# Wide attention of a four-layer block: the order of the front, of the first eight units and of GpSimd's loads rearranged

## The reference

```python
q = rms_norm((x @ wq).reshape(B, L, 16, 128), q_norm_w)
k = rms_norm((x @ wk).reshape(B, L, 4, 128), k_norm_w)
v = (x @ wv).reshape(B, L, 4, 128)
k_ctx = rms_norm((h_ctx_kv @ wk_ctx).reshape(B, T, 4, 128), k_norm_w)
v_ctx = (h_ctx_kv @ wv_ctx).reshape(B, T, 4, 128)
...
```

## Time and profile before

| | |
|---|---|
| median of 3 runs | 1155.62 us (1152.46 to 1157.61) |
| the profiled execution | 1157.82 us, its span 1155.9 us |
| PE busy | 1049.1 us (91%) |
| PE weight loads busy | 847.5 us (73%) |
| DVE busy | 700.8 us (61%) |
| ACT busy | 503.6 us (44%) |
| POOL busy | 232.1 us (20%) |
| mean granted clock of TensorE | 0.972 |

### The profile page before, as it was taken

One profiled execution on the slowest core, in us unless ns is written; L12 is line 12 of the kernel. 1 busy time (PEld: TensorE's weight loads), 2 busy tenths in 40 slices (PEclk: granted clock), 3 DMA queues, 4 the chain that ended last, 5 costly groups with the idle time before them and its releaser, 6 DMA issues.

```text
span 1155.9 us, 23193 instructions
## 1 busy us (share of the span) xinstructions
PE 1049.1 (91%) x9488; PEld 847.5 (73%) x9488; DVE 700.8 (61%) x1337; ACT 503.6 (44%) x867; POOL 232.1 (20%) x356
## 2 busy tenths in 40 slices
PE   6899999989999879999987889989999999999885
PEld 3655678865666645677765668889999999999763
DVE  3646242347777358888643766765665566667466
ACT  3042221125666338888754523333233232232374
POOL 4501038402132000000010411210100133332030
PEclk9998999997999979999999989999999999999898
DMA  9711246554663517000141200131111112100000
GB/s 381 292 72 62 87 153 230 182 140 115 181 180 100 170 39 249 3 2 2 38 147 37 92 25 31 37 110 41 53 37 38 55 58 79 57 19 10 1 2 10
DMA packets 39188, 104.57 MB, mean 90 GB/s; under 512 B 4144, under 2 KB 12720, under 8 KB 37424
## 3 DMA queue, kind: packets, MB, share of 16 engines
q1 hardware_dynamic: 35184, 91.55, 24.2%
q0 software_dynamic: 2752, 9.44, 2.4%
q10 hardware_dynamic: 1152, 2.16, 0.5%
HBM read 87.93 MB, written 15.20 MB: 89 GB/s over the span
## 4 chain that ended last, share of the span: by engine, by line
PE 72%; DVE 13%; ACT 4%; issue 4%; POOL 4%; DMA 2%; DVEq 0%; SPq 0%; POOLq 0%; ACTq 0%
PE ps L2225 9%; PE ps L433 7%; PE ps L2180 7%; PE ps L1413 5%; PE ps L1764 5%; PE ps L426 4%; PE ps L2070 4%; PE ps L488 3%; PE ps L1755 3%; PE ps L1561 3%; PE ps L2084 2%; PE ps L1091 2%; PE ps L1099 2%; PE ps L1572 2%; DVE st L1690 2%
## 5 line engine op out<-in xcount | busy, mean ns | idle before, releaser
L2225 PE MATMUL ps<-vv,prob 128*128 128x129 f32 x1024 | 128.7, 274 | 0.0
L2225 PEld LDWEIGHTS ps<-vv,prob 128*128 128x128 f32 x1024 | 122.5, 192 | 0.0
L1690 DVE TENSOR_REDUCE st<-ps 128x1 f32<-128x512 f32 x128 | 83.5, 687 | 27.3 <-PE ps L1561 21.1
L2348 DVE TENSOR_REDUCE probT<-ps 128x128 f32<-128x1024 f32 x64 | 82.6, 1290 | 28.4 <-PE ps L2180 20.4
L2115 ACT ACTIVATE kt<-ps,w 128x512 f32<-128x512 f32 x32 | 22.1, 689 | 141.8 <-PE ps L2092 141.8
L433 PE MATMUL ps<-xT,big 128*128 128x256 f32 x352 | 79.8, 381 | 1.4 <-ACT xT L715 0.7
L2360 DVE TENSOR_TENSOR prob<-ps,probT 128x1024 f32<-128x1024 f32 x64 | 79.6, 1286 | 1.1
L2321 ACT ACTIVATE prob<-prob 128x1024 f32<-128x1024 f32 x64 | 70.8, 1107 | 19.6 <-DVE prob L2360 19.5
L1637 ACT ACTIVATE prob<-ps 128x1024 f32<-128x1024 f32 x64 | 65.8, 1030 | 28.7 <-PE ps L1572 27.0
L152 POOL TENSOR_SCALAR small<-small 128x4 f32<-128x4 f32 (+1 forms) x44 | 12.0, 273 | 325.7 <-DVE small L2122 175.3
L433 PEld LDWEIGHTS ps<-xT,big 128*128 128x128 f32 x352 | 66.4, 190 | 11.8 <-DVE prob L504 1.9
(11 more groups left out here) (456 smaller groups left out, 2216.1 us busy)
## 6 DMA issues: line engine op xcount, KB each, us to landing
big<-ctxT_in SPq DMA_DIRECT2D x36, 512.0 KB, 4.1
big<-blocks_in SPq DMA_DIRECT2D x22, 768.0 KB, 4.4
key_parts<-w POOLq DMA_DIRECT2D x16, 384.0 KB, 5.0
kt<-key_parts SPq DMA_DIRECT2D x32, 192.0 KB, 3.3
vv<-ctx_in SPq DMA_DIRECT2D x2, 2176.0 KB, 27.3
vv<-early_values SPq DMA_DIRECT2D x4, 1088.0 KB, 12.1
kt<-ctxT_in SPq DMA_DIRECT2D x2, 2048.0 KB, 13.2
kt<-key_parts SPq DMA_DIRECT2D x32, 128.0 KB, 3.2
```

Of the source, the lines that this page charges most:

```text
L1690: dve.tensor_reduce(self.mx[:, u % 2, n:n + 1], k.ps[:, n % 2, :], AX.X, ALU.max).then_inc(s("reduced"), 1)
L2225: last = pe.matmul(k.ps[:, 7, 0:DH + 1], self.prob(u)[:, ch * P:ch * P + P], v, start=(ch == 0), stop=(ch == MC))
L2348: dve.tensor_reduce(self.largest[:, h * P:(h + 1) * P], bank.rearrange("p (c t) -> p t c", t=P), AX.X, ALU.max).then_inc(s("c3_max"), 1)
```

## The change

It touches only the class `Wide` and two functions of `Eight`.

- In the front, key product 4 goes to bank 3 and ahead of the turned keys 0, which move to bank 6; turned heads 4 go ahead of turned keys 2. ScalarE scales heads 1 before the squares 0 and 1; VectorE rotates pieces 3 and 4 earlier and normalizes keys 4 in the front and not in unit 0; GpSimd's order follows.
- In unit 0 turned keys 4 and the projection go ahead of the turning and spreading of the largest scores, the key product behind them; the scores' last four blocks wait for the normalized keys 4 (bank 3).
- In `between_tensor` the values go behind the wait for `w_kt`, and behind the projection where there is one. In units 1 and 4 half of them stay ahead; in TURN_AT's units the turned heads go ahead of the wait; in units 6 and 7 the key product goes ahead of the values.
- ScalarE's order in units 0 to 7 follows (scaling at the unit's start, copy of turned heads behind the key copy, value copy behind the second exp).
- GpSimd's load of the rounded weights' next piece goes behind the root.

```diff
@@ front_tensor
-        self.turn_keys(pe, 0, 3)
-        self.key(pe, 4, 6)
+        self.key(pe, 4, 3)
+        self.turn_keys(pe, 0, 6)
         self.turn_keys(pe, 1, 7)
         pe.wait_ge(s("w_q"), 1)
         self.turn_heads(pe, 0, 3, 0)
-        self.turn_keys(pe, 2, 4)
         pe.wait_ge(s("w_q"), 2)
         self.turn_heads(pe, 0, 4, 1)
+        self.turn_keys(pe, 2, 4)
         self.turn_keys(pe, 3, 5)
@@ scores
+            if u == 0 and ch == 12:
+                pe.wait_ge(s("w_kn"), self.FRONT)
@@ turn_last_output
-        elif u - 1 in self.TURN_AT:
-            pe.wait_ge(s("w_q"), 5 + self.TURN_AT[u - 1] + 1)
@@ between_tensor
-        if g not in self.FIRST_VALUES:
-            self.value(pe, g, 5)
+        if u in self.TURN_AT:
+            self.turn_heads(pe, 1, self.TURN_AT[u], 5)
+        elif u in (1, 4):
+            self.value(pe, g, 5, range(0, 2))
         pe.wait_ge(s("w_kt"), g)
         if u < 6:
             self.project(pe, 1, u, 6)
+        if u == 0:
+            self.turn_largest(pe, u)
+            self.spread_largest(pe, u)
+        if u in (6, 7):
+            self.key(pe, g, 6)
         if u in self.TURN_AT:
-            pe.wait_ge(s("w_v_sb"), g + 1)
-            self.turn_heads(pe, 1, self.TURN_AT[u], 5)
+            pe.wait_ge(s("w_q"), 5 + self.TURN_AT[u] + 1)
+        if u >= 1:
+            self.value(pe, g, 5, range(2, 4) if u in (1, 4) else range(4))
         if u < 6:
             pe.wait_ge(s("w_heads"), 6 + u + 1)
-        self.key(pe, g, 6)
+        if u not in (6, 7):
+            self.key(pe, g, 6)
@@ scalar, the front
+        self.scale_heads(act, 0, 1)
         self.square(act, 0, 6)
         self.square(act, 1, 7)
         self.copy_turned(act, 0, 0, 0)
-        self.scale_heads(act, 0, 1)
-        self.square(act, 2, 4)
         self.copy_turned(act, 0, 1, 1)
         self.scale_heads(act, 0, 2)
+        self.square(act, 2, 4)
         self.square(act, 3, 5)
         self.copy_turned(act, 0, 2, 2)
-        self.copy_keys(act, 0, 3)
         self.scale_heads(act, 0, 3)
-        self.square(act, 4, 6)
+        self.square(act, 4, 3)
+        self.copy_keys(act, 0, 6)
         self.copy_keys(act, 1, 7)
         self.copy_turned(act, 0, 3, 0)
         self.scale_heads(act, 0, 4)
+        self.copy_turned(act, 0, 4, 1)
         self.copy_keys(act, 2, 4)
-        self.copy_turned(act, 0, 4, 1)
         self.copy_keys(act, 3, 5)
@@ scalar, the units
+            if self.TURN_AT.get(u, 0):
+                self.scale_heads(act, 1, self.TURN_AT[u])
             if u >= 2:
                 self.copy_output(act, u - 2, P)
             if g - 1 < self.GROUPS:
                 self.copy_keys(act, g - 1, 6)
-            if self.TURN_AT.get(u, 0):
-                self.scale_heads(act, 1, self.TURN_AT[u])
+            if u in self.TURN_AT:
+                self.copy_turned(act, 1, self.TURN_AT[u], 5)
+            if u == 0:
+                self.copy_heads(act, 1, u, 6)
             if u < self.UNITS:
                 exp(u, 0)
-            if g < self.GROUPS and g not in self.FIRST_VALUES:
+            if u in (6, 7):
+                self.square(act, g, 6)
+            if 1 <= u < 6:
+                self.copy_heads(act, 1, u, 6)
+            if u >= 8 and g < self.GROUPS:
                 self.copy_value(act, g, 5)
             if u < self.UNITS:
                 exp(u, 1)
-            if g < self.GROUPS:
-                if u < 6:
-                    self.copy_heads(act, 1, u, 6)
-                if u in self.TURN_AT:
-                    self.copy_turned(act, 1, self.TURN_AT[u], 5)
+            if 1 <= u < 8:
+                self.copy_value(act, g, 5)
+            if g < self.GROUPS and u not in (6, 7):
                 self.square(act, g, 6)
@@ vector, the front
-        for n in range(3):
+        for n in range(4):
             self.rope(dve, o, 0, n)
         self.sum_squares(dve, 0)
         self.sum_squares(dve, 1)
-        self.rope(dve, o, 0, 3)
+        self.rope(dve, o, 0, 4)
         for g in range(2):
             self.normalize(dve, g, self.key_bank(g))
         self.sum_squares(dve, 2)
         self.sum_squares(dve, 3)
-        self.rope(dve, o, 0, 4)
         for g in range(2, 4):
             self.normalize(dve, g, self.key_bank(g))
         self.sum_squares(dve, 4)
+        self.normalize(dve, 4, self.key_bank(4))
@@ gpsimd
             self.scales(pool, o, g)
+            if u >= self.EIGHT_AT:
+                eight.weights_load(pool, dram, u - self.EIGHT_AT + 2)
```

More of the change, by code:

```diff
@@ L1904 @@
     FIRST_VALUES = (0, 4, 1, 5, 2, 3)
-    KEY_BANKS = (6, 7, 4, 5, 6)
+    KEY_BANKS = (6, 7, 4, 5, 3)
     def __init__(self, k):
@@ L2072, in key, with value @@
         last.then_inc(k.s("w_k"), 1)
-    def value(self, pe, g, bank):
+    def value(self, pe, g, bank, tiles=range(4)):
         k, (b, h, i) = self.k, self.place(g)
@@ L2081, in value @@
         pe.wait_ge(k.s(f"w_stage{slot}"), 16 * loads)
-        for t in range(4):
+        for t in tiles:
             for c in range(DC):
@@ L2085, in value @@
                                  self.ctx("wv_ctx", DC)[:, c, h * DH:(h + 1) * DH], start=(c == 0), stop=(c == 1))
-        last.then_inc(k.s("w_v"), 1)
+        if t == 3:
+            last.then_inc(k.s("w_v"), 1)
     def turn_keys(self, pe, g, bank):
@@ L2275, in tensor @@
                 self.product(pe, u - 1, range(0, 9))
-            if u < self.UNITS:
+            if 1 <= u < self.UNITS:
                 self.turn_largest(pe, u)
@@ L2380, in vector @@
                 self.largest_of(dve, u, 0)
-            if u + F - 1 < self.GROUPS:
+            if F <= u + F - 1 < self.GROUPS:
                 self.normalize(dve, u + F - 1, self.key_bank(u + F - 1))
@@ L2413, in gpsimd @@
         self.ones(pool, o)
-        for n in (1, 2):
+        for n in (1, 2, 3):
             self.query_scales(pool, o, 0, n)
@@ L2417, in gpsimd @@
             self.scales(pool, o, g)
-            if g % 2:
-                self.query_scales(pool, o, 0, 3 + g // 2)
+            if g == 1:
+                self.query_scales(pool, o, 0, 4)
         for g in range(4, self.GROUPS):
@@ L2431, in gpsimd @@
             self.scales(pool, o, g)
+            if u >= self.EIGHT_AT:
+                eight.weights_load(pool, dram, u - self.EIGHT_AT + 2)
         for i in range(self.GROUPS - F - self.EIGHT_AT, eight.PIECES):
             eight.weights_gpsimd(pool, o, dram, i)
+            eight.weights_load(pool, dram, i + 2)
 class Differential:
@@ L2619, in weights_load @@
         s = self.k.s
+        if i >= self.PIECES:
+            return
         if i < 2:
@@ L2632, in weights_gpsimd @@
         pool.tensor_tensor(to, raw, tmp, ALU.subtract).then_inc(s("e8_w"), 1)
-        if i + 2 < self.PIECES:
-            self.weights_load(pool, dram, i + 2)
     TURNED, GATE, UP, MADE = (4, 1), (5, 7, 2, 4), (6, 0, 3, 1), (5, 2)
```

## The result

The changed kernel takes **1163.04 us** (median of 8 runs, 1159.16 to 1167.51) against 1155.7 for the kernel before on the same chips (8 runs): ratio 1.0076, 95% interval 1.0052 to 1.0099, so 6 to 11 us slower. Forecast was 1165.2 with a range of 1158.5 to 1169.5, and slower.

What follows compares the result with a forecast made beforehand. TensorE in wide attention was taken to bound the kernel. Terms 0.65 + 2.5 - 5.35 - 3.1 + 19.95 - 5.1 = +9.55 us, on the median 1155.62, gave 1165.2 us, slower; range 1158.5 to 1169.5.

Steps and rivals of the forecast that it cites:

- The bare wait of units 8 to 26: TensorE's uncovered wait for ScalarE's key copy ahead of the values: 1.05 us a unit, 19.95 us longer in 19 units.
- The rival in which it did not show: Units 8 to 26: the wait costs nothing, the 19.95 us vanish, kernel faster at 1145.2 us; chance 0.1.
- That rival's break-even: Units 8 to 26: wait cost of 0.5 us a unit, below which the change wins.
- The late root: Units 19 to 27: GpSimd's root no longer delays VectorE's largest scores; 9 x 0.57 = 5.1 us shorter.
- The rival of a root that stays late: Units 19 to 27: the 5.1 us are not got back, kernel at 1170.3 us; chance 0.1.
- The front: Before unit 0: key product 4 0.5 us earlier, then scores 8.07 us after it instead of 6.94; 0.65 us longer.
- The clock of the first scores: TensorE's clock falls to its lower level about when scores start: 0 to 3.5 us, taken as 2.5 longer.
- The rival that the clock stays up: First scores: clock does not fall, so without the 2.5 us the kernel takes 1162.7 us; chance 0.2.
- Unit 0: Scores to scores: turned keys 4 and projection fill TensorE's hole; 10.35 us instead of 15.70, 5.35 shorter.
- Units 1 to 7: Work moved into TensorE's waits for ScalarE's copies: 102.9 us instead of 106.04, 3.1 shorter.
- The late largest scores of unit 1: Unit 1: VectorE sums the square of keys 5 late, so the largest scores come 1.5 us late; unit 15.8 us.

Runs made afterwards that it cites:

- experiment 3: The kernel before, with only the values of units 8 to 26 moved behind the wait for the key copy: 1171.28 us, ratio 1.0149 to the kernel before.
- experiment 1: The changed kernel with the values of units 8 to 26 ahead of the wait for the key copy again: 1143.37 us, ratio 0.9897 to the kernel before.
- experiment 4: The kernel before, with only GpSimd's load of the next weight piece moved behind the root: 1149.54 us, ratio 0.9952 to the kernel before.
- experiment 2: Experiment 1 with GpSimd's load ahead of the root again: 1152.39 us, ratio 0.9981 to the kernel before.
- experiment 6: Experiment 1 with the old front's order on all four engines, except that keys 4 are still normalized in the front: 1140.82 us, ratio 0.9878.
- experiment 8: Experiment 1 with ScalarE's scaling of heads 4 ahead of square 4 and key copies, and unit 0's square 5 ahead of both exps: 1139.54 us, ratio 0.9866.

## Why the prediction was right

- **The bare wait of units 8 to 26** was forecast at 19 x 1.05 = 19.95 us from the end of unit 27. It measured 13.47 - 12.41 = 1.06 a unit, 20.1 us, in the changed kernel and in experiment 3, and went with experiment 1. The rival in which it did not show is dead. (That rival's break-even, given as 0.5 us a unit, is 0.55 by the prediction's own terms: the others sum to -10.4, over 19 units.)
- **The late root** was forecast to go either way for 5.1 us. Experiments 3 and 4 show both ways: by the wait alone and by the load alone, 5.3 us in the trace of experiment 4. The credit of 5.1 therefore belongs in the sum of the changed kernel. The prediction gives unit 27 the same 12.99 as the others; it took 10.36 before and 9.77 after, which is the same gain. The rival of a root that stays late is dead too.
- **The front** was forecast 0.65 longer and measured 1.0. Key product 4 came 22.51 us after the first projection (23.12 before), 0.6 earlier for the 0.5 expected. From key product 4 to the scores it took 8.55 where 8.07 was forecast, and the 0.48 more lies behind the turned heads 4, where the turned keys 2 and 3 ran at the low clock.
- **The clock of the first scores** was forecast at 2.5, taken between bounds of 0 and 3.5. It measured 6.02 - 3.84 = 2.2 in the scores and some 0.5 in the turned keys ahead, which is the front's excess above. The rival that the clock stays up fell. All six traces with the wait of 2.26 us for the scaling show first scores slowed, to between 5.56 and 6.29 us; the three with the scaling first and the one with the old front over the new units, where that wait is 1.18 us, have 3.84. That this wait brings this fall is thus shown by what happens when it goes, not only by its place. The Trainium skill's advice ("TensorE: Matmul & The Clock Gate", Why this matters for your kernels), which looks at one long gap, would have missed this fall: the gap was 2.26 us.
- **Unit 0** was forecast 5.35 shorter ahead of the clock: 10.35. Where the clock stays up it takes 10.27 or 10.28. The saving, though, was counted against one execution in which unit 0 held the low clock (15.70). Both new traces of the old order of unit 0 (experiments 3 and 4) show 13.88 there, and in the front

```profile
626.44 12.26 PE L426 MATMUL ps<-big,xT 128*128 128x512 f32 x24 [0.68 <-ACT xT L221]
```

(experiment 4), where the trace of before has 10.57: the low clock came earlier. Against these, unit 0 is only 3.5 us shorter, while their fronts (31.7 and 31.8 us) are longer than the 30.06 of before. From the first projection to the scores of unit 1 the old order takes 45.8, 45.7 and 45.6 us, so in these three the loss moved and did not go, and the sum came right. The prediction gave no reason for that, and it is in part luck: experiment 2 has both the slow projections and the slow first scores (45.6), experiment 6 has neither (40.2).
- **Units 1 to 7** were forecast at 102.9 and measured 102.49. The late largest scores of unit 1 (1.5 forecast, idle 1.17) were the one new wait of TensorE for VectorE among them; it went with experiment 8.
- **The median** came 2 us under the forecast. The stretches sum to +9.1 where +9.55 was said; the rest is outside what was changed, and within the scatter. The forecast difference of 9.55 lies inside the interval of 6 to 11 us, and the runs can tell no more, as those of one version lie 3 to 13 us apart.

## What to carry to other kernels

When a wait is moved past work in a list that several cases share, go through every case: here the values were moved for the first eight units, in which turned heads or half of the values stand ahead of it as cover (unit 0 makes no values), and 19 more units lost their cover with them. The price of such a bare wait can be read where the cover is missing already, at the end of the loop, and the cover need not be all of the work: half of the values took back 0.91 of 1.06 us. Judge an order that touches a short stretch by that stretch's own timeline, since the scatter of the rest is as large as the gain.

## What was not expected

- The load of a weight piece ahead of the root cost 5.4 us alone (experiment 4) and nothing once each unit had 1.06 us to spare (experiment 3).
- The clock's fall under the old order is not tied to one instruction: in one trace it hit the projection of unit 0 (3.78 us for four matmuls), in two others the six projections of the front (12.26 us and not 10.57).
- The start of the front moved by 8.8 us between executions of the same code ahead of it. It goes with the clock there: the two traces with the earliest front (623.05 and 624.99 us) have a mean granted clock of 0.98 over the first 600 us, the two with the latest (631.05 and 631.84) 0.96. What lets the clock fall less in some executions is open.
